# Operand starts at multiples of 128 bytes in the mixing and attention stages of a decoder layer

## What is computed

```python
x = _layernorm(x + mix(x, w_qkv, w_out))      # per head: ifft(cumsum(fft(k) * fft(v)) * conj(fft(q))).real @ w_out
x = _layernorm(x + xattn(x, ctx, mask, ...))  # softmax(where(mask == 0, -1e6, q k^T / sqrt(32))) v @ W_o + b_o
x = _layernorm(x + x @ (int4(kernel)) + bias + (x @ a) @ b)
```

## The kernel before

| operand | role | remainder of 128 |
|---|---|---|
| xT, qT (valsT, oT), w_q, x_tok0, x1 | both stages | 0 |
| w_spec | mixing, stationary | 96 |
| w_back | mixing, moving | 96 |
| x_tok1 | mixing, transposed | 96 |
| k_block, groups 0, 1, 2, 3 | scores, moving | 0, 80, 32, 112 |
| x2T | F, stationary | 64 |
| v_block, pT, w_o, w_ffn | attention | 0 |
| x_res, v_sb, kv, state, qs, vals, r_sb, x1_sb | mixing, DVE, ACT, POOL and DMA | 96 |
| fwd_sb, wT_sb, wqkv_sb, wout_sb, ctxT (chunk 0) | prepare | 96 |

## Time and profile before

### The profile page before, as it was taken

How to read it: one execution, slowest core, us unless ns; L and a number is a source line. 1 busy time by engine, 2 the same in 40 slices (tenths; PEclk the granted TensorE clock), 3 DMA queues, 4 the chain that set the end, 5 groups by cost and what they waited for, 6 DMA issues and landing times.

```text
span 964.6 us, 14638 instructions
## 1 busy us (share of the span) xinstructions
PE 917.6 (95%) x4476; PEld 754.5 (78%) x4476; DVE 666.7 (69%) x1128; ACT 376.8 (39%) x1403; POOL 337.8 (35%) x310
## 2 busy tenths in 40 slices
PE   5898999999999999999779999999999999999987
PEld 4784888888888888888668788888888888888775
DVE  3363466665656565555667888979889798887957
ACT  3152120101010111102287566656567565666610
POOL 2000243232222232324236434444443444433733
PEclk9998999999999999999979999999999999999999
DMA  5944201221203020203423122131222203120021
GB/s 179 326 148 172 90 1 52 80 80 52 104 28 127 3 87 1 88 23 116 134 81 102 25 79 73 40 113 24 89 63 78 75 21 122 30 89 21 17 77 44
DMA packets 72346, 76.02 MB, mean 79 GB/s; under 512 B 38567, under 2 KB 40871, under 8 KB 72303
## 3 DMA queue, kind: packets, MB, share of 16 engines
q1 hardware_dynamic: 72303, 75.49, 24.4%
HBM read 52.60 MB, written 22.87 MB: 78 GB/s over the span
## 4 chain that ended last, share of the span: by engine, by line
PE 41%; DVE 4%; ACT 2%; issue 2%; POOL 2%; POOLq 0%; DVEq 0%
PE shared_ps L74 31%; PE score_ps L74 4%; PE shared_ps L1146 4%; ACT probs L1352 2%; PE shared_ps L1109 1%; PE shared_ps L1179 1%; POOL probs L1501 1%; DVE score_ps L1658 1%; DVE xT_lo L1615 0%; DVE x_and_res L1704 0%; DVE top_s L1663 0%; DVE pT_lo L1642 0%; POOL x_and_res L1516 0%; DVE y L1682 0%; DVE w_o_lo L1825 0%
## 5 line engine op out<-in xcount | busy, mean ns | idle before, releaser
L1352 ACT ACTIVATE probs<-score_ps,top_s 128x77 f32<-128x77 f32 x512 | 159.0, 359 | 36.9 <-DVE top_s L1663 36.9
L1352 ACT ACTIVATION_READ_ACCUMULATOR probs<-score_ps,top_s 128x1 f32 x512 | 122.9, 240 | 0.0
L1501 POOL TENSOR_TENSOR probs<-probs,per_total 128x616 f32<-128x616 f32 x64 | 82.7, 1309 | 65.9 <-DVE per_total L1670 65.7
L1494 POOL TENSOR_TENSOR rstd<-ve,half_power 128x1 f32<-128x1 f32 x64 | 42.4, 662 | 157.1 <-DVE ve L1693 152.5
L722 POOL TENSOR_TENSOR vals<-qs_prod 128x512 f32<-128x512 f32 x32 | 41.1, 1296 | 127.1 <-DVE qs_prod L804 127.1
L713 POOL TENSOR_TENSOR mix_rstd<-mix_ve,half_power 128x1 f32<-128x1 f32 x32 | 22.0, 688 | 175.4 <-DVE mix_ve L823 175.4
L1658 DVE COPY_PREDICATED score_ps<-hidden,masked 128x616 f32<-128x616 int32 x64 | 66.2, 1034 | 11.6 <-PE score_ps L74 11.6
L1359 ACT ACTIVATE pT_hi<-shared_ps 103x512 fp32r<-103x512 f32 (+1 forms) x96 | 54.7, 612 | 46.0 <-PE shared_ps L1146 45.5
L672 ACT ACTIVATE v_sb<-v_ps 128x512 f32<-128x512 f32 x32 | 18.9, 594 | 133.9 <-PE v_ps L74 133.9
L679 ACT ACTIVATE qT_hi<-vals 128x512 fp32r<-128x512 f32 x32 | 19.4, 631 | 122.3 <-POOL vals L722 106.2
L1642 DVE TENSOR_TENSOR pT_lo<-shared_ps,pT_hi 103x512 fp32r<-103x512 f32 (+1 forms) x96 | 64.5, 684 | 0.0
(11 more groups left out here) (218 smaller groups left out, 2660.1 us busy)
## 6 DMA issues: line engine op xcount, KB each, us to landing
x_tok<-in_x SPq DMA_DIRECT2D x8, 1024.0 KB, 5.9
x_res<-in_x SPq DMA_DIRECT2D x8, 1024.0 KB, 8.0
x_between<-mix_x SPq DMA_DIRECT2D x32, 256.0 KB, 2.0
x<-x_between SPq DMA_DIRECT2D x8, 1024.0 KB, 5.5
x_tok<-x_between SPq DMA_DIRECT2D x8, 1024.0 KB, 5.7
out<-y_out SPq DMA_DIRECT2D x32, 256.0 KB, 2.0
wqkv_sb<-in_w_qkv SPq DMA_DIRECT2D x4, 768.0 KB, 7.8
keys_split<-w_q_hi SPq DMA_DIRECT2D x8, 154.0 KB, 5.4
```

The costliest lines, as they stand in the source:

```text
L1352: nc.scalar.activation(probs[:, t % 2, j * KEYS:(j + 1) * KEYS], score_ps[:, g, k * KEYS:(k + 1) * KEYS], ACT.Exp, bias=top[:, t % 2, j:j ...
L1494: nc.gpsimd.tensor_tensor(rstd[:, n:n + 1], ve[:, n:n + 1], half_power[:], ALU.pow).then_inc(rstd_ready, 1)
L1501: nc.gpsimd.tensor_tensor(p, p, per_total[:, t % 2, h * heads:(h + 1) * heads].unsqueeze(2) .to_broadcast([P, heads, KEYS]), ALU.mult).the ...
```

## The change

`mask`, `hidden` and `masked` are allocated in a multiple of 32 words (128 bytes) and used through a view of their former size. The groups of `k_block` are 320 words apart and not 308, and `x2T` begins behind them at word 1280. No instruction is added, removed or moved.

```diff
+LINE = 32
+def up_to_lines(n):
+    return (n + LINE - 1) // LINE * LINE
...
-        keys_end = GROUPS * GK
-        self.k_block = [f[:, 0:keys_end].rearrange("p (g n) -> p g n", g=GROUPS) for f in flat]
-        at = (keys_end + 15) // 16 * 16
+        keys_end = GROUPS * up_to_lines(GK)
+        self.k_block = [f[:, 0:keys_end].rearrange("p (g n) -> p g n", g=GROUPS)[:, :, 0:GK] for f in flat]
+        at = keys_end
         self.x2T = [f[:, at:at + NC * P].rearrange("p (c n) -> p c n", c=NC) for f in flat]
-        self.mask, self.mask_loaded = sb("mask", [P, NT, KEYS], I32), sem("mask_loaded")
+        mask_room = sb("mask", [P, up_to_lines(NT * KEYS)], I32)
+        self.mask, self.mask_loaded = mask_room[:, 0:NT * KEYS].rearrange("p (t k) -> p t k", t=NT), sem("mask_loaded")
...
-        hidden = sb("hidden", [P, NT, KEYS], I32)
-        masked = sb("masked", [P, KEYS])
+        hidden = sb("hidden", [P, up_to_lines(NT * KEYS)], I32)[:, 0:NT * KEYS].rearrange("p (t k) -> p t k", t=NT)
+        masked = sb("masked", [P, up_to_lines(KEYS)])[:, 0:KEYS]
```

## The result

The changed kernel takes 961.1 us, the median of 6 runs (957.93 to 962.12), against 965.13 of the kernel before (6 runs, 964.25 to 966.01): ratio 0.9945, with a 95% interval of 0.9931 to 0.9959. It is faster, by about half of what was forecast: 4.0 us by the two medians, 5.3 us by the ratio and 5.8 us by the two profiled executions, where 10.6 us were forecast; 954.0 and the range up to 958.2 missed it. Timed again, the same file took 960.24 against 966.11, ratio 0.9938 (0.9918 to 0.9957).

A forecast was written before the change was run, and what follows sets the result against it. TensorE's own work was taken to bound mixing, and nearly so attention. Gains of 9.2 us in mixing and 1.4 in F, 10.6 together, off 964.6 gave 954.0 us; range 951.1 to 957.2, or 951.0 to 958.2 with the longer line.

The forecast's parts named there:

- Term 1: Mixing's projections and products back: 1536 matmuls go from 233.3 to 226.7 ns, 10.1 us if all settle at once.
- Term 2: Mixing: settling after 31 breaks at 0.028 us each takes 0.9 us off (0 to 1.6), leaving a gain of 9.2.
- Term 3: Attention's F products with x2T from 64 to 0: 360 matmuls gain 4.3 ns each, 1.4 us after 0.1 off.
- the rival of the longer line: Starts count by 256 bytes: mixing gains 9.2 us, F nothing, O and V lose 2.7; 958.1 us, chance 0.09.
- Terms 4 and 5: Attention's scores from k_block (taken 0, ends 0 and 1.9 us) and the transposes from x_tok1 gain nothing.
- Term 6: Moved operands of DVE, ACT, POOL and DMA in mixing, k_block's clears and prepare's tensors change nothing in the time.
- Term 7: Clock: TensorE reaches attention 9 us earlier; one stretch of lower clock (1.6 us) more or less is possible, none taken.
- The third rival: Attention: TensorE pauses longer before F0 and the probabilities' transposes, the clock falls, 26 us lost; 979 us, chance 0.02.
- The 16-byte line: Part of the no-change rival: with a 16-byte unit the units touched stay the same; 964.6 us, chance of both 0.06.

The follow-up runs named there:

- e8_mix192: `e1_all256` with w_spec, w_back and x_tok1 moved to 192 of 256 bytes, xT and qT staying at 0; 964.15 us in one run.
- e9_mix64: `e1_all256` with w_spec, w_back and x_tok1 moved to 64 of 256 bytes, xT and qT staying at 0; 965.42 us in one run.
- e4_mix128: `e1_all256` with w_spec, w_back and x_tok1 moved to 128 of 256 bytes, xT and qT staying at 0; 964.92 us in one run.
- e3_all96: `e1_all256` with a 24-word pad ahead of w_q, putting every operand of the long products at 96 of 256 bytes; 957.42 us, ratio 0.9908.
- e0_changed: The changed kernel itself, timed and profiled again without any edit; 960.24 us, ratio 0.9938.
- e2_att128: The kernel before with `masked` 32 words longer, so v_block, pT, w_o, w_ffn and probs begin at 128 of 256 bytes; 965.88 us, ratio 0.9995.
- e1_all256: The changed kernel with `masked` 128 bytes longer, so attention's tensors also begin at multiples of 256 bytes; 958.93 us, ratio 0.9917.
- e7_mix_only: `e1_all256` with the old lines of `k_block` and `x2T`, leaving the change's mixing part alone; 958.65 us, ratio 0.9918.
- e10_rows102: `e1_all256` with the 308 keys cut into chunks of 104, 102 and 102 rows, not 103, 103 and 102; 957.22 us in one run.

## Why the prediction was wrong

**The rule itself.** The prediction read "233.3 where one of the operands is off a multiple of 128 bytes, and 226.7 where neither is". What the runs show for 512 columns at clock 1.00, settled:

| d (moving less stationary, mod 256) | ns | where |
|---|---|---|
| 0 | 226.7 | mixing after; all at 96; w_q; O before |
| 32 | 233.3 | w_spec before |
| 64 | 229 or 233, for projections and products back alike | `e8_mix192`, `e9_mix64` |
| 128 | 232.5 to 233.0 | O after; mixing in `e4_mix128` |
| 192 | 233.3 | `e8_mix192`, `e9_mix64` |
| 224 | 233.6 | w_back before |

The 226.7 belongs to operands with the same remainder of 256, and the rest cost 2.5 to 7 ns. (512 isn't the unit: by the allocation w_spec in the changed kernel lies at 256 of 512 from xT, and w_q at 0, and both go 226.7.) The prediction's examples had their aligned operand at 0 of 256 together with its partner, so its own rows could not tell "at a multiple" from "at the same remainder". The closest pair, F2 and F3 of the last step, also differed in a second thing: F2 stands right behind transposes and F3 doesn't. What tells the two readings apart is `e3_all96`: both operands at 96 and 226.7. V doesn't tell them apart, though v_block and pT both went to 128 of 256 and it stayed at 229.8 ns in the steady steps of the profile shown, 229.7 before: with the same starts it goes 230.4 in `e0_changed` and 232.4 in `e2_att128`, and with both at 0 it goes 231.0 in `e1_all256`. The two paces at d = 64 show as well that the difference is not all.

**Term 1, the pace in mixing: right.** 12 starts apart 2.72 us and not 2.80. It was right only because xT and qT lie at 0 of 256 and w_spec and w_back came from 224 to 256, that is 0: at 128, as `e4_mix128` shows, the same words of the change ("a multiple of 128 bytes") would have brought 0.4 us.

**Term 2, the settling: too small.** Mixing gained 8.3 us and not 9.2 (374.8 us also in `e1_all256`, `e7_mix_only` and `e10_rows102`); 10.1 - 8.3 = 1.8 over 31 breaks is 0.058 us each, twice the 0.028 taken, and just over the end of 1.6. The ten matmuls after transposes take 2.32 us against 2.27 settled, and I had put the middle between O3 and O1; O1, behind no break of its own, said nothing of breaks. The prediction named this step as the one at fault if the gain came out smaller; it was one of two.

**Term 3, F: failed, and O with it.** Forecast -1.4 us. F gained 1.4 ns (233.5 to 232.1), O lost 2.9 (229.4 to 232.3), each 48 matmuls a step: +0.07 us a step, and the steady steps went from between 58.68 and 58.75 us to between 58.75 and 58.79. The step of the prediction that failed is its rule of 128 bytes, from which it gave F 4.3 ns each and O and V nothing. This is the rival of the longer line, with its place and sign: it had O at 233.3 and F without gain, and 958.1. It was wrong in two things: V, which was to slow down by some 4 ns, stayed within 0.8 ns in both profiles of the changed kernel, and what counts is not each start by itself. It had 0.09, and the reason against it (32 cycles of surplus fit 32 words) was a match of one number. Aligned to 256, F did gain 3.9 ns, and little of that reached the step.

**Terms 4 and 5, scores and x_tok1: right** as far as can be seen. The scores of the steady steps go 141.3 ns, 141.7 before.

**Term 6: right.** The waits are the same, and DVE's busy time in mixing is 231.97 us.

**Term 7 and what lies around the span.** The start of attention took 1.4 us more in the profile shown, and 0.14 more in the second profile of the same kernel; between kernels alike there it took 44.4 to 47.0. So it isn't shown to be the change's doing, and it can take a good part of a gain of this size in one execution. Over all runs of the two kernels with a recorded span, the median of the changed kernel is 958.6 (12 runs), that of the kernel before 964.3 (35 runs): 5.7 less, as in the two profiles. The mean granted clock of the same runs is 0.979 against 0.981; by a fit of span against clock over all runs some 0.9 us of the missing gain goes with it. Whether the earlier arrival causes that, or chance, stays open. The third rival (979) did not come about: the granted clock of the steady step is 1.00. The prediction also held that under 0.1 us lies around the span; in the median it is 1.9 us (960.67 against 958.8 in the profiled run of the changed kernel). The span of one execution and the times of others had been compared. Made against 964.6 + 1.9, the same sum would have come to 955.9, with a range up to 960.1, which 961.1 misses as well: of the 7.1 us between 954.0 and the measured median, 1.9 are this slip and most of the rest is the missing gain of 4.8.

**The 16-byte line.** The Trainium skill, page "SBUF — State Buffer", in the section "SBUF: two separate sides", speaks of 16-byte cachelines with a penalty for crossing to a new one. By that alone nothing would have changed here, since all starts are multiples of 16: the runs measured 8.3 us in mixing, so it is not what sets this pace.

The sum of the misses, against the profile: settling 0.9, attention's steps 1.9, start of attention 1.4, prepare 0.5, together 4.7 of 4.8 us.

## What to carry to other kernels

Don't align each tensor for itself: give the stationary and the moving operand of a matmul the same start modulo 256 bytes, and check every pair behind a pad, since a pad put in for one product moves those behind it. Here the pad that helped w_spec and w_back set w_o and w_ffn off, and 128 bytes more in one allocation (`e1_all256`) gives them back, with a ratio of 0.9917 against 0.9938 for the change, though the intervals overlap. Before a rule is read from examples, ask whether they differ in one thing only: rows with both operands at 0 can't tell "at 0" from "alike".

## What the runs showed of the hardware that was not expected

- The pace of an fp32r matmul of 512 columns at clock 1.00 depends on the two operands' starts relative to each other: 226.7 ns with the same remainder of 256 bytes, whichever it is (0 or 96), and up to 233.6 otherwise. At d = 64 the same kind of matmul goes at 229 in one place and at 233 in another of one trace (`e8_mix192`, `e9_mix64`), and it keeps its pace until the next break or product of another kind; at d = 192 it always goes 233.3.
- Behind transposes, or behind a change of the number of rows, an aligned stream begins at the slower pace and takes some ten matmuls to reach 226.7; ten take 2.31 to 2.32 us and not 2.27. It can take longer: in one steady step of `e2_att128` the last 27 matmuls of V (from 643 us) never settle, 232.5 on average, where they take 228.9 in the kernel before. Moving `ident` doesn't remove it (2.29 to 2.31 us). What it is stays open.
- A stretch of lower clock comes and goes between executions of one kernel, and costs 1.5 to 1.7 us where it falls (`e0_changed` against the first profile: 376.48 and 374.82 us of mixing).
- The stage in which attention starts takes 44.4 to 47.0 us in kernels that are alike there, 1.3 us apart in two profiles of one kernel.
- Open too: what chooses between the two paces at d = 64, and why V in the steady steps goes from 229.7 to 232.4 ns between kernels in which both of its operands start alike.
